# Eight heads to one bank of weighted values, and a new order of all engines with a period of one visit

## The chip, the core and the metric

The kernel runs on one core of a Trainium2 chip. The metric is the device time in microseconds (us) from the first to the last instruction; the median of three runs before the change is 2798.29 us. The engines are PE (TensorE, matmuls), ACT (ScalarE), DVE (VectorE), POOL (GpSimd) and SP (SyncE, which here only issues DMAs). Each works through its own instructions in program order and waits on semaphores.

## What is computed

A small network over x (4 batches, 512 tokens, 128 features): slot attention, a mixture of experts, six transformer layers and a quantised feed-forward block, each added to x. The change touches the six layers alone, and in them mostly the two attentions (16 heads of 8 features; 512 tokens on themselves, then on 77 context rows):

```python
def _attn(q, k, v, mask):
    scores = jnp.einsum('bqhd,bkhd->bhqk', q, k) / np.float32(np.sqrt(HD))
    scores = jnp.where(mask[:, None, None, :], jnp.float32(-jnp.inf), scores)
    w = jax.nn.softmax(scores, axis=-1)
    return jnp.einsum('bhqk,bkhd->bqhd', w, v)
...
for i in range(NL):
    xn = _adaln(x, noise_emb, n1_w[i], n1_b[i])
    ...
    a = _attn(q, k, v, src_mask).reshape(B, L, D) @ so_w[i].T
    x = x + a
    ...
    a = _attn(q, k, v, ctx_mask).reshape(B, L, D) @ co_w[i].T
    x = x + a
    xn = _adaln(x, noise_emb, n3_w[i], n3_b[i])
    h = jax.nn.gelu(xn @ f1_w[i].T + f1_b[i], approximate=False)
    x = x + (h @ f2_w[i].T + f2_b[i])
```

## The kernel before

The function `layers` (from L836) does the six layers for four batches: 24 visits, visit v being layer v // 4 and batch v % 4. One visit has, for the self-attention:

- "product query", "product key" (L1168): the rows of the normalised x times the weights, then DVE turns them (L1475), POOL and ACT split the float32 result into three bfloat16 parts (POOL "rotate" L1394, ACT "first" L1305, POOL "less" L1399, ACT "second" L1310, POOL "third" L1405). SP writes the parts to DRAM ("store", L651 to L661) and reads them back in another arrangement ("load pairs", L953 to L956: per half of the partitions the queries, the keys and the mask row) into `q6` and `k6`, which have two buffers, one for each of two neighbouring visits.
- "PE max" (L1039), 32 places of two matmuls each: scores with the queries on the rows, of which DVE takes the maximum of each row (L1450). The first of a visit waits for that visit's load of pairs. A group of four heads ("unit") has eight of them; POOL splits its maxima ("split", L1409 to L1412), PE turns them (L1105), ACT copies them (L1273) and SP puts them as rows into `q6` ("SP rows", L980).
- "PE exp" (L1050), 32 places of two matmuls: scores with the keys on the rows, less the maxima. ACT takes the exponential into `probs` (L1259).
- "PE pv" (L1086): four matmuls, one a head, of the weights times the values with a column of ones behind them. Each head writes 32 partitions of bank 6 (`pv_bank`), of which 9 hold something. After four such places a group of four heads is done: ACT copies the bank ("copy", L1267), PE turns it ("gather", L1122, four transposes), DVE inverts the sums and multiplies (L1482, L1487). There are four units a visit.
- "turn on", "project" (L1129, L1138), "DVE add" (L1493): the output projection.

The cross-attention has the same steps with 8 places of scores, 8 of maxima and 4 of "cross pv" (L1097, into bank 7, called `aux`), each of these with its own copy, gather and division. Then comes the feed-forward part ("up" L1192, "gelu" L1331, "down" L1201). Once a layer the keys of the context are made ("product context" L1168, "rope context" L1471, ... "store context"), and SP loads them with eight DMAs ("load context", L974), and the layer's weights come in.

The order of all engines is a table of numbers, `OFFSETS` (L674), one number for each place of an operation, repeated with the period `PERIOD` (here 15124 for two visits); `LAYER_OFFSETS` (L776) does the same once a layer. Every engine's instructions are written in rising order of these numbers, and semaphores make each wait for what it needs, so the table sets only the order on each engine. The same numbers, taken as times, hand out the buffers through `shared` (L824): three pairs of PSUM banks for the scores and products, three buffers of `probs` of four heads each (`QUAD_BUFFERS`), two of the copied bank.

## Time and profile before

| | before |
|---|---|
| median of three runs | 2798.29 us (2793.4 to 2815.2) |
| time of the profiled execution | 2804.61 us |
| its span, first to last instruction | 2802.5 us |
| PE busy | 2148.6 us (77%) |
| DVE busy | 1811.4 us (65%) |
| ACT busy | 1588.6 us (57%) |
| POOL busy | 907.6 us (32%) |
| mean granted clock of PE | 0.887 |

The first 550 us are slots, routing and experts, the last 155 the quantised block; neither is changed. The layers run from about 550 to 2645 us. In the page's 40 slices PE is busy nine tenths or more in nearly all of them from the tenth slice to the last but five, with a granted clock of nine tenths. A busy share is read as the time in which at least one matmul was under way; where two lines of a timeline overlap, the distance of their starts says what the first one cost. In a timeline the bracket at a line's end is the time that the engine stood idle before it, and what released it.

### The profile page before, as it was taken

What the parts mean: (1) busy time and instruction counts of PE and PEld (TensorE: products, weight loads), DVE (VectorE), ACT (ScalarE), POOL (GpSimd) and SP (SyncE); (2) the same over time, 40 slices, a digit from 0 to 9 for tenths busy, and PEclk for the clock granted to TensorE, in tenths of its full rate; (3) what the DMA queues carried; (4) which work ended last, traced back from release to release, by engine and by line L of the source; (5) the groups of instructions that cost most, each with busy time, mean ns of one, the idle gap of its engine ahead of it and who ended that gap; (6) DMA issues with size and microseconds to landing.
All of it is one profiled execution on the core that took longest, in us unless ns stands there. A gap on an engine that the chain in (4) does not pass through costs nothing. (4 is left out here: it accounts for less than half of the span.)

```text
span 2802.5 us, 40867 instructions
## 1 busy us (share of the span) xinstructions
PE 2148.6 (77%) x14402; PEld 947.5 (34%) x14402; DVE 1811.4 (65%) x3776; ACT 1588.6 (57%) x2003; POOL 907.6 (32%) x1951
## 2 busy tenths in 40 slices
PE   2444799637789988999899998999899998986312
PEld 1223466511233333333333333333333333332101
DVE  6777211335677776776777777777677777652398
ACT  2221233105577776677777776777677776773223
POOL 4110000032244344443443353444344343322133
PEclk9665899857899999999999999999999999997655
DMA  1000000022322332233333313332342223310000
GB/s 42 0 0 0 31 13 18 26 52 47 79 72 59 70 80 76 48 69 75 69 82 70 69 54 75 77 70 64 66 97 62 55 52 87 70 25 24 23 0 15
DMA packets 141019, 144.47 MB, mean 52 GB/s; under 512 B 30808, under 2 KB 122644, under 8 KB 140820
## 3 DMA queue, kind: packets, MB, share of 16 engines
q1 hardware_dynamic: 140831, 142.05, 22.1%
q8 instruction: 109, 1.79, 0.3%
q14 instruction: 79, 0.64, 0.1%
HBM read 79.01 MB, written 60.51 MB: 50 GB/s over the span
## 5 line engine op out<-in xcount | busy, mean ns | idle before, releaser
L1259 ACT ACTIVATE big<-ps 128x1024 f32<-128x1024 f32 x960 | 969.4, 1025 | 374.1 <-PE ps L1050 348.1
L1450 DVE TENSOR_REDUCE smax<-ps 128x2 f32<-128x1024 f32 x768 | 916.4, 1219 | 235.6 <-PE ps L1039 233.3
L1086 PE MATMUL ps<-big,vaug 128*32 128x512 f32 x3072 | 421.5, 621 | 4.0 <-ACT big L1259 3.8
L1039 PE MATMUL ps<-k,q 49*128 49x512 bf16 x1536 | 303.0, 398 | 156.1 <-DVE smax L1450 70.5
L1050 PE MATMUL ps<-q,k 52*128 52x512 bf16 x1536 | 305.0, 397 | 31.3 <-ACT big L1259 18.5
L1394 POOL TENSOR_TENSOR rot<-rot 128x512 f32<-128x512 f32 (+1 forms) x78 | 96.5, 1237 | 510.3 <-DVE rot L1471 366.5
L1039 PEld LDWEIGHTS ps<-k,q 49*128 49x128 bf16 x1536 | 73.2, 94 | 395.6 <-DVE smax L1450 148.4
L1457 DVE TENSOR_REDUCE maxima<-ps 128x8 f32<-128x616 f32 x192 | 149.3, 796 | 72.5 <-PE ps L1073 71.2
L1168 PE MATMUL ps<-xnT,w 128*128 128x512 f32 x288 | 167.5, 668 | 2.2 <-ACT xnT L1296 1.7
L624 DVE SCALAR_TENSOR_TENSOR state<-ps,share,state 128x128 f32<-128x128 f32 x128 | 36.0, 344 | 201.7 <-PE ps L595 201.7
L612 ACT ACTIVATE big<-ps 128x512 f32<-128x512 f32 x128 | 76.4, 597 | 144.3 <-PE ps L586 144.3
L1475 DVE TENSOR_TENSOR rot<-ps,cs 128x1024 f32<-128x1024 f32 x72 | 88.1, 1223 | 103.5 <-PE ps L1168 103.5
L1493 DVE TENSOR_TENSOR state<-state,ps 128x512 f32<-128x512 f32 x72 | 49.6, 688 | 154.4 <-PE ps L1201 98.6
L1050 PEld LDWEIGHTS ps<-q,k 52*128 52x128 bf16 x1536 | 75.4, 94 | 215.7 <-issue 77.4
L586 PE MATMUL ps<-xnT,big 128*128 128x512 f32 x256 | 119.0, 610 | 24.8 <-DMA big<-in_c_proj 24.8
L1409 POOL CAST mparts<-smax 128x16 bf16<-128x16 f32 x96 | 19.1, 199 | 362.7 <-DVE smax L1450 362.7
L1122 PE MATMUL ps<-ident,xnT 128*128 128x128 f32 x768 | 126.2, 288 | 11.9 <-ACT xnT L1267 8.8
L1267 ACT COPY xnT<-ps 128x512 f32<-128x512 f32 x192 | 112.5, 586 | 33.7 <-PE ps L1097 23.4
L1201 PE MATMUL ps<-w,big 128*128 128x128 f32 x768 | 126.5, 317 | 4.0 <-ACT big L1331 4.0
L595 PEld LDWEIGHTS ps<-big 128*128 128x128 f32 x1024 | 119.1, 192 | 14.3 <-issue 14.3
L595 PE MATMUL ps<-big 128*128 128x128 f32 x1024 | 119.2, 275 | 0.0
L1201 PEld LDWEIGHTS ps<-w,big 128*128 128x128 f32 x768 | 108.5, 219 | 29.3 <-issue 21.3
(274 smaller groups left out, 3252.5 us busy)
## 6 DMA issues: line engine op xcount, KB each, us to landing
q<-scratch_queries SPq DMA_DIRECT2D x48, 384.0 KB
k<-scratch_keys SPq DMA_DIRECT2D x48, 384.0 KB
cq<-scratch_cross_queries SPq DMA_DIRECT2D x48, 384.0 KB, 5.5
scratch_queries<-rparts SPq DMA_DIRECT2D x24, 384.0 KB, 2.3
scratch_keys<-rparts SPq DMA_DIRECT2D x24, 384.0 KB, 2.5
scratch_cross_queries<-rparts SPq DMA_DIRECT2D x24, 384.0 KB, 2.3
scratch_queries<-rparts SPq DMA_DIRECT2D x24, 256.0 KB, 2.6
scratch_keys<-rparts SPq DMA_DIRECT2D x24, 256.0 KB, 2.7
```

What stands on the lines that cost most here:

```text
L586: nc.tensor.matmul(m.ps[:, n % 4, :], m.fc[:, u, c * P:(c + 1) * P], m.xnT[:, b, :], start=True, stop=True).then_inc(h_ps, 1)
L595: last = nc.tensor.matmul(m.ps[:, 4 + i % 2, t * P:(t + 1) * P], m.hT[:, i % 2, c, t * P:(t + 1) * P], m.proj[:, u, c, :], start=(c == 0), ...
L1039: last = nc.tensor.matmul(out[:, u], m.q6[rows, v % 2, 2 * g + pr, qt * P:(qt + 1) * P], m.k6[rows, v % 2, 2 * g + pr, :], start=True, sto ...
L1050: last = nc.tensor.matmul(out[:, u], m.k6[rows, v % 2, 2 * g + pr, kt * P:(kt + 1) * P], m.q6[rows, v % 2, 2 * g + pr, :], start=True, sto ...
L1086: last = nc.tensor.matmul(m.ps[32 * j:32 * j + 32, pv_bank, :], m.vaug[:, v % 2, kt, 4 * g + j, :], of_quad("self", q)[:, j, :], start=(kt ...
L1122: last = nc.tensor.transpose(m.ps[:, aux, t * P:(t + 1) * P], m.unit[:, unit[kind, n], t * P:(t + 1) * P], m.ident[:])
L1168: got = nc.tensor.matmul(banks(kind, i)[:, half, 0:width(kind)], w_of(m, names[half]), rhs, start=True, stop=True)
L1201: last = nc.tensor.matmul(m.ps[:, aux, t * P:(t + 1) * P], m.hT1[:, c, t * P:(t + 1) * P], w_of(m, "f2")[:, c * P:(c + 1) * P], start=(c = ...
L1259: nc.scalar.activation(of_quad(kind, p // 2)[:, p % 2 * 2:p % 2 * 2 + 2, :], banks("exp" if kind == "self" else "cross exp", p), ACT.Exp, ...
L1267: nc.scalar.copy(m.unit[:, unit[kind, n], :], m.ps[:, pv_bank if kind == "self" else aux, :]).then_inc(u_sb[kind], 1)
L1450: nc.vector.tensor_reduce(m.smax[:, n % 2, qt, :, pr], banks("max", i), AX.X, ALU.max).then_inc(s_read["self"], 1)
L1457: nc.vector.tensor_reduce(m.maxima[:, qt, :, PAIRS // 2 * half:PAIRS // 2 * (half + 1)], banks("cross max", i)[:, :, 0:PAIRS // 2 * N_CTX] ...
```

## The change

Eight heads share the bank of weighted values. A head's own 32 columns are 16 zeros, 8 of values, the column of ones and 7 zeros. A head of an even group uses the 32 columns that begin at its values, so its result lies in rows 0 to 8 of 32 partitions and zeros are added to rows 16 to 31; a head of an odd group uses those that begin 16 before its values, so its result lies in rows 16 to 24. Both add into the same 32 partitions. So bank 6 is copied, turned and divided once for two groups: two units a visit in place of four, for the self-attention and the cross-attention alike. The rows of the projection weights `so` and `co` are permuted on the host to fit. The division works on twice as many columns.

`QUAD_BUFFERS` goes from 3 to 4, `hT1` gets memory of its own, and the context's keys get buffers of their own (`rot_c`, `rparts_c`, `left_c`); their product is made in two halves in bank `aux`, behind visit 0's first work and no longer ahead of everything. The period is one visit, 7218, and all numbers of the table are new.

```diff
-PERIOD_VISITS = 2
-PERIOD = 15124
+PERIOD_VISITS = 1
+PERIOD = 7218
 OFFSETS = {
...
     "PE max": (
-        -4847, -4662, -4608, -4142, -4025, -3873, -3726, -3639, -3501, -3362, -3205, -2802, -2623, -2444, -2265, -1004, -675, -555, -370,
...
+        -4361, -4115, -3949, -3669, -3607, -3448, -3299, -3248, -2981, -2752, -2226, -1995, -1972, -1842, -1644, -1514, -1042, -77, 114,
...
-    "ACT second key": (-6597, 903),
+    "ACT second key": (-5775,),
-    "SP load pairs": (-5986, 1514),
+    "SP load pairs": (-5161,),
...
-QUAD_BUFFERS = 3
+QUAD_BUFFERS = 4
+UNIT_PAIRS = GROUPS // 2
...
+    def of_head(values, block, g, j):
+
+        at = (block * HEADS + 4 * g + j) * 32 + 16 * (1 - g % 2)
+        return values[:, at:at + 32]
...
-                if kt == 0 and n >= 1:
-                    pe.wait_ge(u_sb["self"], n)
+                if kt == 0 and g % 2 == 0 and n >= 2:
+                    pe.wait_ge(u_sb["self"], n // 2)
                 for j in range(4):
-                    last = nc.tensor.matmul(m.ps[32 * j:32 * j + 32, pv_bank, :], m.vaug[:, v % 2, kt, 4 * g + j, :], of_quad("self", q)[:, j, :],
-                                            start=(kt == 0), stop=(kt == TB - 1))
+                    last = nc.tensor.matmul(m.ps[32 * j:32 * j + 32, pv_bank, :], of_head(m.vaug, v % 2 * TB + kt, g, j),
+                                            of_quad("self", q)[:, j, :], start=(kt == 0 and g % 2 == 0), stop=(kt == TB - 1 and g % 2 == 1))
...
             def copy_unit(kind, n):
-                act.wait_ge(pv[kind], TB * (n + 1) if kind == "self" else n + 1)
+                act.wait_ge(pv[kind], 2 * (n + 1) * (TB if kind == "self" else 1))
...
             def turn_on(kind, v):
-                pe.wait_ge(on[kind], GROUPS * (v + 1))
+                pe.wait_ge(on[kind], UNIT_PAIRS * (v + 1))
...
+            def context_products(half, n):
+                weights("context", n)
+                take_aux(x_read["context"], 2 * n + half + 1)
+                for k, name in enumerate(("ck", "ckr")):
+                    last = nc.tensor.matmul(m.ps[:, aux, k * N_HALF:(k + 1) * N_HALF], w_of(m, name),
+                                            m.ctxT[:, half * N_HALF:(half + 1) * N_HALF], start=True, stop=True)
+                last.then_inc(x_ps["context"], 1)
```

On PE, in the cross-attention of one visit in the middle of the layers, the program before has this order (`big,vcaug` is "cross pv", `ident,xnT` a gather, `cq,kc` and `q,k` scores for the exponential, `k,q` scores for the maxima):

```order
L1097 MATMUL ps<-big,vcaug 32x512 x4
L1039 MATMUL ps<-k,q 128x512 x2
L1061 MATMUL ps<-cq,kc 128x512 x2
L1122 MATMUL ps<-ident,xnT 128x128 x4
L1039 MATMUL ps<-k,q 128x512 x2
L1061 MATMUL ps<-cq,kc 128x512 x2
L1097 MATMUL ps<-big,vcaug 32x512 x4
L1039 MATMUL ps<-k,q 128x512 x2
L1061 MATMUL ps<-cq,kc 128x512 x4
L1122 MATMUL ps<-ident,xnT 128x128 x4
```

Every weighting is followed by its own gather, with scores between them. The same place of the changed program, on PE:

```order
L1103 MATMUL ps<-big,vcaug 32x512 x4
L1066 MATMUL ps<-cq,kc 128x512 x2
L1044 MATMUL ps<-k,q 128x512 x2
L1103 MATMUL ps<-big,vcaug 32x512 x4
L1044 MATMUL ps<-k,q 128x512 x2
L1055 MATMUL ps<-q,k 128x512 x2
L1128 MATMUL ps<-ident,xnT 128x128 x4
L1066 MATMUL ps<-cq,kc 128x512 x2
```

Two weightings share a gather; single pairs of scores still stand between them. On PE just ahead of the first maxima of a visit (the instruction that names `pairs_loaded`), before; here the semaphores that an instruction waits for stand behind it:

```order
L1050 MATMUL ps<-q,k 128x512 [waits max_read_self]
L1050 MATMUL ps<-q,k 128x512
L1039 MATMUL ps<-k,q 128x512 [waits probs_self]
L1039 MATMUL ps<-k,q 128x512
L1050 MATMUL ps<-q,k 128x512 [waits max_read_self]
L1050 MATMUL ps<-q,k 128x512
L1138 MATMUL ps<-w,on 128x128 [waits rows_copied_cross,weights_out]
L1138 MATMUL ps<-w,on 128x128 x3
L1039 MATMUL ps<-k,q 128x512 [waits max_read_self,pairs_loaded_0]
L1039 MATMUL ps<-k,q 128x512
L1050 MATMUL ps<-q,k 128x512 [waits probs_self]
L1050 MATMUL ps<-q,k 128x512
```

The first maxima stand behind the cross-attention's projection. The same place of the changed program, on PE:

```order
L1055 MATMUL ps<-q,k 128x512 [waits probs_self]
L1055 MATMUL ps<-q,k 128x512
L1144 MATMUL ps<-w,on 128x128 [waits rows_copied_cross,weights_out]
L1144 MATMUL ps<-w,on 128x128 x3
L1055 MATMUL ps<-q,k 128x512 [waits probs_self]
L1055 MATMUL ps<-q,k 128x512
L1091 MATMUL ps<-big,vaug 32x512 [waits probs_self]
L1091 MATMUL ps<-big,vaug 32x512 x3
L1044 MATMUL ps<-k,q 128x512 [waits max_read_self,pairs_loaded_0]
L1044 MATMUL ps<-k,q 128x512
L1055 MATMUL ps<-q,k 128x512 [waits probs_self]
L1055 MATMUL ps<-q,k 128x512
```

They stand one pair of scores and one weighting behind the projection; the wait for the pairs is on them in both. The third place is on ACT, from the second cast of the keys (`rparts<-hat`, "ACT second key"), before:

```order
L1259 ACTIVATE big<-ps 128x1024 [waits weighted_self,scores_cross]
L1310 CAST rparts<-hat 128x512 [waits less_high_key]
L1267 COPY xnT<-ps 128x512 [waits unit_turned_self,weighted_cross]
L1259 ACTIVATE big<-ps 128x1024 [waits scores_cross]
L1259 ACTIVATE big<-ps 128x1024 [waits weighted_self,scores_cross]
L1259 ACTIVATE big<-ps 128x1024 [waits scores_cross]
L1267 COPY xnT<-ps 128x512 [waits unit_turned_self,weighted_cross]
L1259 ACTIVATE big<-ps 128x1024 [waits weighted_cross,scores_cross]
```

The cast stands behind the second exponential of the cross-attention (`scores_cross`) and ahead of its four copies. On ACT in the changed program:

```order
L1270 ACTIVATE big<-ps 128x1024 [waits weighted_self,scores_cross]
L1278 COPY xnT<-ps 128x512 [waits unit_turned_self,weighted_cross]
L1270 ACTIVATE big<-ps 128x1024 [waits scores_self]
L1322 CAST rparts<-hat 128x512 [waits less_high_key]
L1270 ACTIVATE big<-ps 128x1024 [waits scores_cross]
L1270 ACTIVATE big<-ps 128x1024 [waits weighted_cross,scores_cross]
L1270 ACTIVATE big<-ps 128x1024 [waits scores_cross]
L1270 ACTIVATE big<-ps 128x1024 [waits weighted_cross,scores_self]
```

The cast has moved behind the first of the (now two) copies, deeper into the cross-attention, and less work stands between it and the first maxima.

## Rows read from the trace of the kernel before

**Rows 1.** Busy time by engine in the full part of the layers (us, instructions in brackets):

```profile
840.00:2500.00 1660.00, 1500.77 (x10850) 589.76 (x10848) 1214.76 (x2005) 1213.99 (x1483) 680.83 (x1620) 0.97 0.30 67
```

**Rows 2.** Waits of PE, 946 to 2391 us: us in total, times, longest:

```profile
PE ps L1039 <- DVE smax L1450: 44.9, 83, 1.6
PE ps L1039 <- DMA k<-scratch_neg_mask: 27.0, 9, 5.1
```

**Rows 3.** ACT's timeline, copies of the values of visits 5 and 23 (start, us, instruction):

```profile
946.96 0.59 ACT L1316 COPY vaug<-ps 128x512 f32<-128x512 f32 x1 [1.44 <-PE ps L1175]
...
2391.21 0.59 ACT L1316 COPY vaug<-ps 128x512 f32<-128x512 f32 x1 [1.44 <-PE ps L1175]
```

**Rows 4.** PE's timeline, five neighbours of one piece:

```profile
1207.94 0.39 PE L1050 MATMUL ps<-q,k 52*128 52x512 bf16 x2
1208.16 0.38 PE L1039 MATMUL ps<-k,q 49*128 49x512 bf16 x2
1208.47 1.07 PE L1086 MATMUL ps<-big,vaug 128*32 128x512 f32 x8
1209.47 0.66 PE L1122 MATMUL ps<-ident,xnT 128*128 128x128 f32 x4
1210.06 0.39 PE L1050 MATMUL ps<-q,k 52*128 52x512 bf16 x2
```

**Rows 5.** The page's groups of instructions: gathers on PE, copies on ACT:

```profile
L1122 PE MATMUL ps<-ident,xnT 128*128 128x128 f32 x768 | 126.2, 288 | 11.9 <-ACT xnT L1267 8.8
L1267 ACT COPY xnT<-ps 128x512 f32<-128x512 f32 x192 | 112.5, 586 | 33.7 <-PE ps L1097 23.4
```

**Rows 6.** Timelines, visit 9: second cast of keys, first load, first maxima:

```profile
1271.59 0.62 ACT L1310 CAST rparts<-hat 128x512 bf16<-128x512 f32 x1
...
1277.00 0.33 SPq L953 DMA_DIRECT2D q<-scratch_queries  x1
...
1290.25 0.39 PE L1039 MATMUL ps<-k,q 49*128 49x512 bf16 x2 [0.84 <-DMA k<-scratch_neg_mask]
```

**Rows 7.** Windows within that load; the last two columns are DMA share, GB/s:

```profile
1282.00:1284.00 2.00, 2.00 (x18) 1.08 (x12) 0.93 (x2) 0.90 (x1) 0.00 (x0) 1.00 1.13 155
```

**Rows 8.** Timelines, visit 8, whose first maxima follow no wait:

```profile
1195.38 0.62 ACT L1310 CAST rparts<-hat 128x512 bf16<-128x512 f32 x1
...
1214.20 0.39 PE L1039 MATMUL ps<-k,q 49*128 49x512 bf16 x2
```

**Rows 9.** Timelines, visit 10, with the context's load ahead of the pairs':

```profile
1352.46 0.62 ACT L1310 CAST rparts<-hat 128x512 bf16<-128x512 f32 x1
...
1358.41 4.91 SPq L974 DMA_DIRECT2D kc<-scratch_ctx_keys  x8
1363.43 0.41 SPq L953 DMA_DIRECT2D q<-scratch_queries  x1
...
1376.06 0.61 PE L1039 MATMUL ps<-k,q 49*128 49x512 bf16 x2 [4.83 <-DMA k<-scratch_neg_mask]
```

**Rows 10.** Windows after the waits of visits 1, 6, 10; third number from the end: clock:

```profile
662.00:672.00 10.00, 7.57 (x52) 1.90 (x52) 4.85 (x4) 4.71 (x6) 0.00 (x0) 0.83 0.01 2
1052.00:1062.00 10.00, 8.84 (x44) 2.68 (x44) 5.15 (x14) 4.88 (x6) 1.45 (x8) 0.68 0.02 3
1376.00:1386.00 10.00, 9.94 (x56) 3.25 (x60) 6.64 (x17) 5.81 (x7) 2.61 (x13) 0.83 0.01 3
```

**Rows 11.** Timelines, first work of the layers, first maxima, last visit's first maxima, last addition:

```profile
555.84 2.42 PE L1168 MATMUL ps<-ctxT,w 128*128 128x308 f32 x4 [21.69 <-DMA w<-in_w]
...
559.34 0.86 DVE L1505 BATCH_NORM_STATS2 bn_next<-state 128x6 f32<-128x128 f32 x4
...
600.87 1.46 PE L1039 MATMUL ps<-k,q 49*128 49x512 bf16 x6 [22.08 <-DMA k<-scratch_neg_mask]
...
2414.65 0.39 PE L1039 MATMUL ps<-k,q 49*128 49x512 bf16 x2 [0.59 <-ACT big L1259]
...
2644.21 0.69 DVE L1493 TENSOR_TENSOR state<-state,ps 128x512 f32<-128x512 f32 x1 [20.06 <-PE ps L1201]
```

More of the change, by code:

```diff
@@ L790 @@
[L790 to L799 removed]
+    "SP weights self": 3476,
+    "PE gain cross": 4223,
+    "DVE gain cross": 4268,
+    "SP weights out": 9987,
+    "SP weights ff": 13180,
+    "PE gain ff": 13780,
@@ new lines @@
+    "DVE gain ff": 13825,
+    "SP weights next": -10281,
+    "PE gain next": -8458,
+    "DVE gain next": -8413,
+    "PE context values": 10506,
+    "ACT copy context values": 10616,
+    "SP load context": 8933,
+    "SP weights context": 5188,
+    "PE product context 0": 6688,
+    "DVE rope context 0": 6773,
+    "PE product context 1": 7018,
+    "DVE rope context 1": 7103,
+    "POOL rotate context": 7198,
+    "ACT first context": 7358,
+    "POOL less context": 7458,
+    "ACT second context": 7598,
@@ L800 @@
+    "POOL third context": 7698,
+    "SP store context": 7838,
 }
```

339 lines of the change are left out of this document (167 added, 172 removed), and 21 rows, old and new, of the table OFFSETS.

## The prediction

> **What bounds the kernel now.** I read the busy shares first. In the full part of the layers PE is busy for 1500.8 of 1660 us, 90%, DVE and ACT for 73% each [rows 1]. So PE sets the pace, and what counts is what PE does and what it waits for. The copies of the values of visit 5 and visit 23 are 1444.25 us apart [rows 3], 18 visits, so a visit takes 80.24 us. The table has 75.62 for it (half of 15124, if its numbers count 10 ns; that they do is shown below).
>
> Then the waits of PE. In the 1445 us it stood for DVE's maxima 44.9 us in 83 small pieces, and 27.0 us in only 9 pieces for the DMAs of the pairs [rows 2]. The second kind matters here. After the second cast of the keys comes a fixed chain: last part, store, load, first maxima. In visit 9 the cast starts at 1271.59, SP issues the load at 1277.00 (5.41 later), and PE's first maxima come at 1290.25, 13.25 after the issue, with 0.84 of waiting [rows 6]. So the load takes some 13 us until PE may go on; while it runs the queues are full, a DMA share of 1.13 at 155 GB/s [rows 7]. In visit 10 it is 12.63 us from 1363.43 to 1376.06 [rows 9]. Cast to first maxima thus needs 5.41 + 12.6 to 13.25, so **18.0 to 18.7 us**. The table of before leaves 17.84 us between these two places in odd visits (2687 less 903, in units of 10 ns) and PE reached the place 18.66 - 0.84 = 17.82 us after the cast: the table's numbers are times of 10 ns, and PE keeps them where nothing holds it. Before, the load is just covered.
>
> Once a layer SP has the context's eight loads ahead (4.91 us to issue), the load goes out 10.97 us after the cast, and PE waits 4.83 us [rows 9].
>
> **The change part by part.**
>
> *Gathers.* 24 visits x 4 gathers fall away. One costs 0.59 us to the next start, and the pair of scores ahead of it 0.31 in place of 0.22 [rows 4]: 0.68 x 4 = 2.7 us of PE a visit. Over the program this is 65 us; the page's 126.2 us for 768 transposes give 63 for half of them [rows 5].
>
> *Matmuls side by side.* The extra 0.1 us is paid where scores (bfloat16, on half the rows) meet another kind. In the order there are 959 places on PE where scores are followed by something else, 876 after. That is 83 fewer, and the 96 gathers alone would remove up to 96. So the new order in itself saves nothing here.
>
> *ACT and DVE.* 96 copies of 0.586 us go [rows 5], and half of the inversions and products, whose remaining ones are twice as wide. Both engines have a quarter of their time free, so I price this at nothing; if ACT or DVE set the pace it would be worth 2.3 us a visit at the most.
>
> *More buffers, the context in two halves.* The fourth buffer of `probs` and the memory for `hT1` remove waits of ACT, which isn't the bound. The context's matmuls are 24 of half the width in place of 12. Nothing, either way.
>
> *The table.* 75.62 - 72.18 = 3.44 us a visit: 2.7 are the gathers, 0.7 tighter packing. I take all of it, since what made 80.24 of 75.62 (once-a-layer work that the period doesn't hold, the clock, waits) mostly stays.
>
> *What the table takes away.* It leaves 5775 - 4361 = 1414, 14.1 us, from the second cast of the keys to the first maxima, where 17.5 to 17.8 stood. The order says why this is real: between the scores of the exponential ahead of the cast and the first maxima, PE had 25 pairs of scores, 7 weightings, 4 gathers, a transpose group and a projection (visit 9), and now has 20, 6, 2, 1 and 1. By rows 4 that is 5 x 0.22 + 1.00 + 2 x 0.59 = 3.3 us less, 3.7 with the switches. The cast can't come earlier: it stands on ACT behind exponentials and a copy that wait for PE. Nor can the load: SP waits for the stores, as before. So the data are there 18.0 to 18.7 us after the cast and PE 14.1 us after: a **new wait of 3.9 to 4.6 us in every visit**. Visit 8 reached its place 18.82 us after the cast without waiting where the table had 17.50 [rows 8], 1.3 us late, so the wait may be as short as 2.6. I take 3.9. Everything of PE stands behind it, so ACT, DVE and POOL stop too.
>
> In the visit with the context's loads these can start once the last cross scores are done, 2.1 us after the cast by the table, plus an exponential, plus 4.9 of issuing: the pairs go out some 8 us after the cast, 2.6 later than in others. That wait is about 6.0. The mean is (3 x 3.9 + 6.0) / 4 = 4.4 us.
>
> *The clock.* In the 10 us behind such waits the mean granted clock was 0.83 (visit 1), 0.68 (visit 6) and 0.83 (visit 10, after 4.83 us of waiting) [rows 10]. It has two levels, 2.4 GHz (1.0) and 1.2 GHz (0.5), so it was at the lower one for 3.4, 6.4 and 3.4 us, in which half the work of PE is lost: 1.7 to 3.2 us. I take 2.1 a wait. The Trainium skill, "TensorE: Matmul & The Clock Gate", section "HAM oscillation — how this bites in real kernels", says that a kernel which waits for a DMA in every tile pays the fall of the clock in every tile. The trace agrees for these three waits.
>
> *Taken away with the old table.* The old waits: 4.8 and some 2.3 of clock a layer, and 0.3 a visit (3.4 us in four such pieces are what rows 2 hold beside the layers' 23.6): 2.1 a visit.
>
> A visit: 80.24 - 3.44 - 2.1 + 4.4 + 2.1 = **81.2 us**, 0.96 more. From the first maxima to those of the last visit there are 23 (600.87 to 2414.65 [rows 11]), so +22 us.
>
> *Ends.* The first statistics of the layers stood behind the context's product and its turning, until 559.34 [rows 11]; now they don't: between nothing and the 9 us since the stage began, I take 5 (the product alone is 2.42). From the last visit's first maxima to the last addition the table has 259.1 us and now 246.9; measured are 230.3 [rows 11], so 12.2 x 0.89 = 11 us fewer.
>
> **Sum.** 2804.6 (the profiled execution) - 5 + 22 - 11 = 2810.6. The median lies 6.3 below that execution: **2804 us**. About 1% is what a measurement of this kernel can tell from no change, that is 2770 to 2826.
>
> **Rivals.**
>
> *The load stays hidden: faster.* Then a visit is 80.24 - 3.44 - 2.1 = 74.7 us and the program 2798 - 16 - 23 x 5.5 = 2655 us. It needs PE to be 4 us late between cast and maxima, or a load of under 9 us. Against it: the load took 12.6 us or more with full queues [rows 7, 9]. Chance 0.15. The Trainium skill, "DMA: Bandwidth & Descriptors", section "Anatomy of one DMA — SWDGE (gpsimd) path", fits a DMA as 2.0 us and its bytes at 436 GB/s. The four large loads of 48x8x512 bfloat16 are 1.57 MB: an estimate of 5.6 us by that page, which would be hidden. The trace has 13 and less than half that rate.
>
> *The wait comes, but cheaper: faster.* It is 2.6 to 3.5 us long, the clock mostly holds, or PE's later waits for DVE and ACT shrink by as much since these have caught up. A visit is 80.24 - 5.54 + 3.4 to 4.4, so 78.1 to 79.1, and the program 2733 to 2756. For it: 45 us of small waits for maxima [rows 2]. Against it: PE keeps the table's distances (17.82 us against 17.84), so they hold little slack to win back. Chance 0.2.
>
> *A second wait: slower.* SP's rows of maxima for the third unit now stand 3.0 us (3288 to 3588) ahead of the scores that need them, where 5.2 stood. If these small DMAs take 4 us or more and land behind the pairs' traffic, PE waits another 1 us a visit; with the full 3.2 of clock and waits of 4.8 a visit is 80.24 - 5.54 + 4.8 + 3.2 + 1.0 = 83.7 and the program 2798 - 16 + 23 x 3.5 = 2862. It decides from a rows' landing of 3.0 us on. Chance 0.15.
>
> **How the numbers follow.** The forecast as summed has 0.5, with its own range of 2770 to 2850 (wait 2.9 to 4.6, clock 1.7 to 3.2). Of it 0.35 lie within 1% and 0.15 above. Faster by over 1%: 0.15 + 0.2 = 0.35. Within 1%: 0.35. Slower by over 1%: 0.15 + 0.15 = 0.30. The range 2725 to 2855 holds the forecast and the cheaper wait and leaves out the hidden load and most of the second wait.
>
> **What will show it.** Right: PE's wait for `k<-scratch_neg_mask` has some 24 pieces of 3 to 6 us, near 100 us in all; the first maxima come 12.5 to 13.3 us after the load's issue; the clock is at 0.5 behind most of them; gathers are 384 transposes, 63 us; visits are 80 to 82 us apart. Wrong: such waits under 1.5 us (the load was hidden, or PE late for another reason), visits of 75 us, or a large wait for the DMA of the rows of maxima.

## The result and the profile after

| | before | after |
|---|---|---|
| median of the runs, us | 2799.5 (20 runs, 2789.2 to 2815.2) | 2784.4 (20 runs, 2777.5 to 2797.1) |
| ratio, 95% interval | 1 | 0.9945 [0.9932, 0.9958] |
| profiled execution, us | 2802.5 | 2776.6 |
| mean granted clock | 0.887 | 0.868 |
| copies of values, visit 5 to 23, us | 1444.25 | 1444.35 |

The changed kernel is 0.55% faster: inside the range and inside "within 1%", but on the other side of no change than the forecast of 2804. The steady visit came out at the 80.24 us of before, where I had 81.2. That it is the same to the hundredth is an accident of sums that cancel, as the experiments show; the gain lies at the two ends.

The groups of instructions for gathers and for the copies that feed them (line, engine, operation | busy us, mean ns | idle before). They answer to [rows 5]:

```profile
L1128 PE MATMUL ps<-ident,xnT 128*128 128x128 f32 x384 | 62.2, 285 | 14.4 <-ACT xnT L1278 8.8 <-ACT mct L1290 5.6
L1278 ACT COPY xnT<-ps 128x512 f32<-128x512 f32 x96 | 56.4, 588 | 26.1 <-PE ps L1091 17.9 <-PE ps L1103 8.2
```

Half of both is gone: 384 transposes, 62.2 us, as forecast (63).

PE's waits, 978 to 2423 us, the 18 visits from 5 to 23 (in total, times, longest), against [rows 2]:

```profile
PE ps L1044 <- DMA k<-scratch_neg_mask: 105.5, 18, 9.2
PE ps L1044 <- DVE smax L1460: 21.8, 36, 0.9
PE ps L1111 <- DVE on_rows L1499: 18.0, 18, 1.0
```

The new wait is there, once in each of the 18 visits, 5.9 us in the mean (forecast 4.4). But the small waits for DVE's maxima, 44.9 us in 83 pieces before, are 21.8 in 36, and two more of before, 946 to 2391 us, are gone from this list, the scores' waits for ACT's gelu and for its exponentials:

```profile
PE ps L1039 <- ACT big L1331: 13.7, 27, 0.8
PE ps L1050 <- ACT big L1259: 12.8, 40, 0.6
```

Without the waits for the load PE was idle for 112.0 us in these 18 visits before (139.0 less 27.0) and for 59.4 us after (164.9 less 105.5). One new small wait has come: the turn of maxima stands right behind a gather and waits 1.0 us for DVE's products.

One such wait, visit 11. Timelines of ACT, SP and PE (start, us):

```profile
1425.85 0.61 ACT L1322 CAST rparts<-hat 128x512 bf16<-128x512 f32 x1
...
1428.66 0.51 SPq L661 DMA_DIRECT2D scratch_keys<-rparts  x1
...
1433.24 0.32 SPq L958 DMA_DIRECT2D q<-scratch_queries  x1
...
1446.04 0.61 PE L1044 MATMUL ps<-k,q 49*128 49x512 bf16 x2 [6.37 <-DMA k<-scratch_neg_mask]
```

PE reached the place at 1446.04 - 6.37 = 1439.67, 13.82 us after the cast (forecast 14.1), and the load took 12.80 us from its issue (forecast 12.6 to 13.25). What I had too short in this visit is the way from cast to load: 7.39 here, 5.41 in my sum. The windows over this wait (PE busy, clock, DMA share, GB/s):

```profile
1442.00:1444.00 2.00, 0.00 (x0) 0.99 1.13 144
1444.00:1446.00 2.00, 0.00 (x0) 0.50 0.22 29
1446.00:1448.00 2.00, 1.97 (x8) 0.50 0.00 0
1448.00:1450.00 2.00, 2.00 (x11) 0.50 0.00 0
1450.00:1452.00 2.00, 2.00 (x12) 0.80 0.01 4
```

PE stands, the clock falls from 2.4 to 1.2 GHz, and PE's work begins at the lower one and keeps it for some 5 us. In the 2 us behind each of the 18 waits the mean granted clock was 0.50 to 0.55, and 8 us behind them it was back at 1.00.

The first and the last visit's first maxima and the last addition, against [rows 11]:

```profile
594.27 1.46 PE L1044 MATMUL ps<-k,q 49*128 49x512 bf16 x6 [25.44 <-DMA k<-scratch_neg_mask]
...
2407.84 0.60 PE L1044 MATMUL ps<-k,q 49*128 49x512 bf16 x2 [6.01 <-DMA k<-scratch_neg_mask]
...
2618.30 0.69 DVE L1505 TENSOR_TENSOR state<-state,ps 128x512 f32<-128x512 f32 x1 [18.50 <-PE ps L1210]
```

Head: 600.87 to 594.27, 6.6 us earlier (forecast 5). Between the two first maxima: 1813.6, before 1813.8. Tail: 210.5 us where 229.6 stood, 19.1 less (forecast 11).

### The profile page after: what moved, and what is told of

It reads as the page before. It is cut to its first block and busy times, and to the rows that moved or that the text cites. A ratio compares the mean times of both kernels' runs of the same rounds, so it can differ in the third digit from the quotient of the medians.

```text
span 2776.6 us, 39486 instructions
## 1 busy us (share of the span) xinstructions
PE 2102.3 (76%) x14041; PEld 910.0 (33%) x14042; DVE 1790.8 (64%) x3584; ACT 1526.3 (55%) x1907; POOL 906.5 (33%) x1951
## 5 line engine op out<-in xcount | busy, mean ns | idle before, releaser
L1270 ACT ACTIVATE big<-ps 128x1024 f32<-128x1024 f32 x960 | 947.7, 1023 | 383.2 <-PE ps L1055 358.8
L1044 PE MATMUL ps<-k,q 49*128 49x512 bf16 x1536 | 310.2, 407 | 194.8 <-DMA k<-scratch_neg_mask 155.1
L1091 PE MATMUL ps<-big,vaug 128*32 128x512 f32 x3072 | 427.5, 636 | 2.1 <-ACT xnT L1278 1.8
L1406 POOL TENSOR_TENSOR rot<-rot 128x512 f32<-128x512 f32 x72 | 91.4, 1269 | 186.9 <-DVE rot L1476 186.8
L1390 POOL TENSOR_TENSOR tmp_next<-rstd_next 128x4 f32<-128x4 f32 x72 | 14.2, 198 | 365.5 <-DVE rstd_next L1529 361.8
L1210 PE MATMUL ps<-w,hT 128*128 128x128 f32 x768 | 129.0, 321 | 2.4 <-ACT hT L1343 2.4
L1284 ACT COPY mt<-ps 12x512 bf16<-12x512 bf16 x96 | 55.1, 574 | 130.5 <-PE ps L1111 130.5
L1210 PEld LDWEIGHTS ps<-w,hT 128*128 128x128 f32 x768 | 109.9, 221 | 44.8 <-issue 40.4
L595 PEld LDWEIGHTS ps<-big 128*128 128x128 f32 x1024 | 119.1, 192 | 14.3 <-issue 14.3
L1416 POOL TENSOR_TENSOR rparts<-hat,rparts 128x512 bf16<-128x512 f32 x72 | 83.4, 1158 | 113.3 <-ACT rparts L1322 113.3
L1410 POOL TENSOR_TENSOR hat<-rot,rparts 128x512 f32<-128x512 f32 x72 | 83.5, 1160 | 110.6 <-ACT rparts L1318 110.6
```

The source lines that it names most:

```text
L595: last = nc.tensor.matmul(m.ps[:, 4 + i % 2, t * P:(t + 1) * P], m.hT[:, i % 2, c, t * P:(t + 1) * P], m.proj[:, u, c, :], start=(c == 0), ...
L1044: last = nc.tensor.matmul(out[:, u], m.q6[rows, v % 2, 2 * g + pr, qt * P:(qt + 1) * P], m.k6[rows, v % 2, 2 * g + pr, :], start=True, sto ...
L1091: last = nc.tensor.matmul(m.ps[32 * j:32 * j + 32, pv_bank, :], of_head(m.vaug, v % 2 * TB + kt, g, j), of_quad("self", q)[:, j, :], start ...
L1210: last = nc.tensor.matmul(m.ps[:, aux, t * P:(t + 1) * P], m.hT1[:, c, t * P:(t + 1) * P], w_of(m, "f2")[:, c * P:(c + 1) * P], start=(c = ...
L1270: nc.scalar.activation(of_quad(kind, p // 2)[:, p % 2 * 2:p % 2 * 2 + 2, :], banks("exp" if kind == "self" else "cross exp", p), ACT.Exp, ...
L1406: nc.gpsimd.tensor_tensor(x[:, 0, :], x[:, 0, :], x[:, 1, :], ALU.add).then_inc(x_rot[kind], 1)
```

## The experiments

Times are medians; ratios are against the kernel before, run on the same chip in the same job, so they compare across jobs. "Visit" is the distance of ACT's copies of values from visit 5 to visit 23, by 18. PE busy and idle and the mean granted clock are of those same 18 visits. With the merge that is the same work of PE in every kernel but `fill` and the padded ones, which add some.

| run | median us | ratio [95%] | visit us | PE busy, idle us | clock |
|---|---|---|---|---|---|
| before | 2799.5 | 1 | 80.24 | 1305.2, 139.0 | 0.97 |
| after | 2784.4 | 0.9945 [0.9932, 0.9958] | 80.24 | 1279.5, 164.9 | 0.93 |
| later300 | 2763.3 | 0.9847 [0.9818, 0.9877] | 79.81 | 1284.8, 151.8 | 0.95 |
| later600 | 2710.3 | 0.9661 [0.9630, 0.9691] | 77.02 | 1261.4, 125.0 | 0.98 |
| half_load | 2628.0 | 0.9370 [0.9342, 0.9398] | 72.94 | 1242.5, 70.4 | 0.98 |
| fill | 2760.6 | 0.9827 [0.9781, 0.9872] | 79.00 | 1305.6, 116.3 | 0.96 |
| split4 | 2619.1 | 0.9356 [0.9320, 0.9392] | 73.20 | 1242.2, 75.4 | 0.98 |
| before_split4 | 2756.5 | 0.9829 [0.9779, 0.9879] | 78.43 | 1297.7, 114.0 | 0.98 |
| ctx_after | 2768.0 (one run) | none | 79.41 | 1281.8, 147.6 | 0.94 |
| merge_old_table | 2841.3 | 1.0130 [1.0090, 1.0171] | 82.74 | 1308.4, 181.0 | 0.94 |
| merge2 | 2880.9 | 1.0275 [1.0231, 1.0318] | 84.29 | 1312.2, 205.0 | 0.93 |
| merge2_split4 | 2830.9 | 1.0086 [1.0053, 1.0119] | 82.49 | 1302.8, 182.1 | 0.94 |
| merge3_split4 | 2768.2 | 0.9882 [0.9862, 0.9902] | 79.48 | 1273.6, 157.0 | 0.96 |
| merge3_pad | 2801.1 | 1.0002 [0.9987, 1.0018] | 80.28 | 1299.7, 145.4 | 0.97 |
| split4_pad | 2653.8 | 0.9460 [0.9436, 0.9485] | 74.96 | 1280.1, 69.3 | 0.98 |
| split2 | 2597.4 | 0.9265 [0.9231, 0.9299] | 72.36 | 1242.1, 60.4 | 0.98 |
| best1 | 2591.3 | 0.9245 [0.9211, 0.9280] | 71.89 | 1234.8, 59.2 | 0.99 |
| best2 | 2601.9 | 0.9278 [0.9253, 0.9304] | 72.43 | 1242.4, 61.4 | 0.98 |

### Is the wait for the load paid, or do other waits take its place?

Theory A says that the wait is paid in full; theory B, that without it other waits would stand in its place. First the place of the maxima was moved, in the table only. `later600` (`later300` alike with some 280 units):

```diff
     "PE max": (
-        -4361, -4115, -3949, -3669, -3607, -3448, -3299, -3248, -2981, -2752, -2226, ...
+        -3750, -3524, -3344, -3087, -3026, -2829, -2724, -2668, -2529, -2416, -2073, ...
-    "POOL split": (-3002, -1323, 1636, 2753),
+    "POOL split": (-2402, -1323, 1636, 2753),
```

> The changed kernel with only the first ten blocks of maxima of a visit placed later: 0 to 7 by about 280 units (3.2 us at 80.24 us per 7218 units), 8 by 180, the reading on DVE, the first split on POOL with them; nothing else is moved. Their place on PE comes after other matmuls of the period, so that PE reaches the wait for the loaded pairs later. Theory A (the wait of 5.8 us for the load is paid in full in each visit, and a clock loss behind it): the wait shrinks by about 3 us in 23 visits, 2784 - 70 = about 2715, and less if the clock stays up. Theory B (PE's waits are interchangeable: what the load wait does not take, waits for DVE's reading or for the exponentials take, as the 80.24 us per visit both kernels show suggests): within 10 us of 2784.

> The same with the first eight blocks of maxima placed about 590 units (6.5 us) later, and 8 to 10 by 450, 340 and 150, so that they stand close together. Theory A: the load wait (mean 5.8 us in 18 visits, 6.7 to 9.2 us in the context visits) is all but gone except in the visits that load the context; 23 x 5.8 = 133 us, with the clock after the wait (about 2 us a visit) up to 180: 2600 to 2650. Theory B: the maxima, now packed, wait for DVE's reading (1.2 us each) instead: within 15 us of 2784.

PE's waits of later600, visits 5 to 23:

```profile
PE ps L1036 <- DVE smax L1452: 44.7, 54, 1.3
PE ps L1047 <- DVE smax L1452: 19.9, 18, 1.1
PE ps L1036 <- DMA k<-scratch_neg_mask: 8.1, 7, 2.1
```

The load wait went from 105.5 to 8.1 us and the clock from 0.93 to 0.98, yet the visit gave back 3.2 us, not 7: maxima that stand close together wait for DVE's reading, 64.6 us where 21.8 stood, and a matmul of the feed-forward part ("down") waits 13.6 us for ACT's copy of the turned maxima. In later300 the load wait fell by 43 us, but 14.3 us of waits for an exponential and 7 for DVE came, PE was busy 5 us more, and the visit gained 0.4. Neither theory is right alone: the wait is paid, and this way of hiding it costs half or more of its worth. The next run leaves the order alone and makes the load shorter.

```diff
-                    sp.dma_start(m.q6[lo:lo + ROW_MASK, i], src[u]).then_inc(loaded[i], 16)
+                    few = PAIRS if v < 2 else PAIRS // 2
+                    sp.dma_start(m.q6[lo:lo + ROW_MASK, i, 0:few], src[u][:, 0:few]).then_inc(loaded[i], 16)
...
-                    sp.dma_start(m.k6[lo:lo + ROW_MASK, i], src[u]).then_inc(loaded[i], 16)
+                    sp.dma_start(m.k6[lo:lo + ROW_MASK, i, 0:few], src[u][:, 0:few]).then_inc(loaded[i], 16)
```

> The changed kernel with the order untouched, but from the third visit on each of the four large transfers of queries and keys moves pairs 0 to 3 only, half of its bytes; pairs 4 to 7 keep what an earlier visit left, so this part of the attention is computed on old data. Theory A: the load, 12.3 to 13.3 us from issue to first maxima, takes about 7.5 us; the wait of 5.8 us falls to 1 or less in ordinary visits: 22 x 5 = 110 us, 2670, less still with the clock. Theory B: the wait disappears, and the time stays within 15 us of 2784.

2628 us, ratio 0.937, even below theory A's figure: a visit almost without the wait takes 72.94 us, where my sum had 74.7. PE's waits of half_load, visits 5 to 23:

```profile
PE ps L1037 <- DVE smax L1453: 21.8, 36, 0.9
PE ps L1104 <- DVE on_rows L1492: 18.0, 18, 1.0
PE ps L1037 <- DMA k<-scratch_neg_mask: 11.0, 6, 3.0
```

The small waits are those of the changed kernel to the tenth: the long wait didn't cover or shrink them, it stood beside them. Theory B falls.

`fill` asks for the clock's part:

```diff
+FILL = 11
...
+                out = free_banks("max", i)
                 if i % PER_VISIT == 0:
+                    if v >= 2:
+                        for k in range(FILL):
+                            for u in range(2):
+                                rows = slice(u * ROW_BLOCK, u * ROW_BLOCK + ROWS_MAX)
+                                nc.tensor.matmul(out[:, u], m.q6[rows, 1 - v % 2, k % PAIRS, 0:P], m.k6[rows, 1 - v % 2, k % PAIRS, :],
+                                                 start=True, stop=True)
                     pe.wait_ge(loaded[v % 2], 96 * (v // 2 + 1))
```

> The changed kernel with 11 pairs of matmuls more ahead of each wait for the load (22 of 49 x 128 by 512 columns, about 4.5 us a visit), repeating maxima of the visit before into the bank that the first maxima then overwrite: PE is busy in the time in which it waited. It tells the clock's share from the wait's. If the lower clock behind the wait costs 2.1 us a visit as I took it (23 visits): 2784 - 45 = about 2740, with the granted clock over the steady stretch up from 0.93 to 0.97. If the clock would have fallen anyway, or what it costs is hidden by other waits: 2780 to 2800, the fill costing a little in the visits where it runs past the load.

It gained 1.2 us a visit without making anything else shorter; the clock rose from 0.93 to 0.96, and 56.5 us of the wait stayed, 3.1 a time. So work that nobody reads buys back part of the clock's cost, about half of what I forecast; half of the wait was still there, and with it a stretch at the lower clock.

`split4` is `half_load` without leaving anything out, and `before_split4` the same edit in the kernel before:

```diff
+FIRST_PAIRS = 4
...
+                for part, done in ((slice(0, FIRST_PAIRS), loaded[i]), (slice(FIRST_PAIRS, PAIRS), late[i])):
+                    for u in range(2):
...
+                        sp.dma_start(m.q6[lo:lo + ROW_MASK, i, part], src[u][:, part]).then_inc(done, 16)
...
+                        sp.dma_start(m.k6[lo:lo + ROW_MASK, i, part], src[u][:, part]).then_inc(done, 16)
...
+                if i % PER_VISIT == FIRST_PAIRS // 2 * PER_UNIT:
+                    pe.wait_ge(late[v % 2], 64 * (v // 2 + 1))
```

> The changed kernel with each load of pairs cut in two: the pairs 0 to 3 of queries and keys and the mask first, then pairs 4 to 7, each part with a semaphore of its own; the first maxima wait for the first part, the maxima of group 2 (about 50 us later) for the second. All bytes move, the computation is whole, the order on the engines is untouched. Theory A, by the run with half of the load (72.9 us a visit, first maxima no longer late): the wait of 5.8 us goes in the same way; the four issues more on SP's queue and the second half's traffic beside it take a little back: 2630 to 2660. Theory B (it was the halved traffic of that run, less contention for all transfers, that made it fast): 2720 to 2780.

> The kernel before with the same cut of the load in two. Its table gives the load 18.0 to 18.7 us, and PE waited for it 27.0 us in 9 of 18 visits. If the load was nearly hidden there, the cut is worth these waits and the clock behind them, 30 to 40 us: 2799 - 35 = about 2765. If cutting the load helps by itself, in traffic or for SP's queue, it gains as much as in the changed kernel, 120 us or more.

2619 us with all bytes moved: what PE paid for was the time until the first pairs are there. The windows over the 18 visits of after and of split4 (PE, PEld, DVE, ACT, POOL busy, clock, DMA share, GB/s):

```profile
978.31:2422.66 1444.35, 1279.50 (x9137) 490.08 (x9136) 1044.05 (x1605) 1008.59 (x1221) 602.40 (x1420) 0.93 0.33 70
```

```profile
939.51:2257.12 1317.61, 1242.19 (x9137) 481.97 (x9136) 1043.27 (x1605) 1006.15 (x1221) 604.48 (x1420) 0.98 0.35 77
```

The same 9137 matmuls in the same order. Of the 126.7 us between the two, 89.4 are idle time of PE (the load wait went from 105.5 to 15.5) and 37.3 are PE busy longer with the same work, at a mean granted clock of 0.93 in place of 0.98. That is 5.0 us of wait and **2.1 us of clock** for each visit, the price that I had taken from three windows. `split2` below, in which 1.0 us of the load wait is left, has 5.8 and 2.1: the whole new wait costs 7.9 us a visit. In the kernel before the same cut gave 1.8 us a visit (forecast of the old wait: 2.1) and 1.7%, no more.

The Trainium skill, "TensorE: Matmul & The Clock Gate", section "HAM oscillation — how this bites in real kernels", says that a kernel which waits for a DMA in each tile pays a throttled stretch behind each wait; its example has 1.67 us of it, half of that lost. This trace agrees on the mechanism, 18 times in 18 visits, and has 2.1 us lost each time.

```diff
-    "SP load context": 8933,
+    "SP load context": 9400,
```

> The changed kernel with the load of the context's keys, eight transfers, placed 225 units later, behind the load of pairs of the same visit in place of ahead of it. Theory A (the waits of 6.7 to 9.2 us in visits 6, 14, 18 and 22 are longer by the context's transfers ahead of the pairs): these fall to 4 to 6 us, the sum of the waits in 18 visits from 104 to about 93 us, the time by 10 to 15 us. Rival: they stay as they are, since the stores and the load of the cross queries, not the context, hold the queues.

PE's waits of ctx_after, visits 5 to 23:

```profile
PE ps L1036 <- DMA k<-scratch_neg_mask: 88.2, 18, 6.3
```

From 105.5 to 88.2 us, the longest from 9.2 to 6.3. In the five visits that load the context the wait fell from 8.1 to 5.1 us in the mean; in the other 13 it stayed near 5. It was the context's transfers. The time is of one run only and has no interval.

### What are the gathers worth, and what the new order?

The merge alone: the changed kernel with the old table, of which each pair's second place was kept for copy, gather and division.

```diff
-PERIOD_VISITS = 1
-PERIOD = 7218
+PERIOD_VISITS = 2
+PERIOD = 15124
...
```

> The merge alone: the changed kernel (eight heads into one bank, half of the copies, gathers and divisions) under the table of the kernel before, in a period of two visits, with the second place of each pair kept for copy, gather and division; one first block of the context's weighted values and the two products of the context stand a little elsewhere, since they share the auxiliary bank. There the load has 18 us and is waited for 1.5 us a visit. Theory A, my sum's term: 2.7 us of PE a visit for the gathers that fall away, in 24 visits: 2800 - 62 = about 2740, still 80.24 - 2.7 = 77.5 us a visit. Rival: the gathers lay in time in which PE would have waited for DVE or ACT anyway: within 15 us of 2800.

> The merge alone under the table of the kernel before, as in the run merge_old_table, with the load cut in two as in split4 and the context's two products placed so that neither waits for the other's reading (in merge_old_table PE waited 1.7 us there, and its clock was 0.50 for 10 us behind it, once in four visits). Beside the kernel before with the cut load (2756 us, 78.4 us a visit) it is the merge without any load wait. If the gathers' 2.7 us of PE a visit are worth their time when nothing stalls: 2756 - 62 = about 2695. If they only turn into other waits under this table: within 15 us of 2756. What is left to 2619 us, the changed kernel with the cut load, is then the new table's.

> The merge alone under the old table with the whole load in one, and the context's products placed as in merge2_split4. If the misplaced context products made merge_old_table slow (2841 us; the visits with them took 86.6 us in place of 81.0, so 6 x 5.6 = 34 us), this gives about 2805, no faster than the kernel before; if my term of 2.7 us a visit holds besides, about 2745.

All three are slower than the kernel before or than its version with the cut load. The misplaced context products don't explain it as I thought: at the new places of merge2,

```diff
-    "PE product context 0": -17520,
+    "PE product context 0": -17420,
...
-    "PE product context 1": -17225,
+    "PE product context 1": -16690,
```

it got worse (2881 against 2841 us). PE now waited 11.2 us in 4 pieces for the reading of these products, 9.5 in 8 before: in the auxiliary bank each half holds up the bank's next user. The scores' waits for exponentials grew more, from 17.6 to 36.9 us, the longest from 1.0 to 5.2. Windows of merge2_split4 at one place, PE idle and the clock lower behind it (PE busy, clock, DMA share, GB/s):

```profile
1281.77:1285.77 4.00, 3.47 (x26) 1.00 0.66 210
1285.77:1289.77 4.00, 2.09 (x14) 0.73 1.06 190
1289.77:1293.77 4.00, 4.00 (x18) 0.50 1.15 171
```

These windows led me to theory C: gathers that fall away turn into waits and a lower clock. For a clean test the context's products went back to the ring of banks and their old places, and in the padded kernels as much work as the gathers had was put in:

```diff
-                take_aux(x_read["context"], 2 * n + half + 1)
+                if half == 0:
+                    free_banks("context", n)
...
-                    last = nc.tensor.matmul(m.ps[:, aux, k * N_HALF:(k + 1) * N_HALF], w_of(m, name),
+                    last = nc.tensor.matmul(banks("context", n)[:, half, k * N_HALF:(k + 1) * N_HALF], w_of(m, name),
...
+            def pad():
+                if reader[0] is not None:
+                    pe.wait_ge(*reader[0])
+                for t in range(TB):
+                    nc.tensor.transpose(m.ps[:, aux, t * P:(t + 1) * P], m.ident[:], m.ident[:])
...
+                if kt == TB - 1 and g % 2 == 0:
+                    pad()
...
+                if g % 2 == 0:
+                    pad()
```

> The merge alone under the old table with the load cut in two, as merge2_split4, but the context's products keep their ring bank and their old places, so that the context visits (84.5 us there against 73.8) are as in the kernel before with the cut load (2756 us). My term: the gathers are worth 2.7 us a visit, about 2695. Theory C, from the trace of merge2_split4 (at a place where two gathers stood, PE now waited 2.1 us more for DVE's readings, and the clock fell to 0.50 to 0.73 for 5 us behind it): the old table has DVE and ACT one step behind PE, so gathers that fall away turn into waits and lower clock, 2750 to 2790.

> merge3_split4 with the PE work of the removed gathers put back: four transposes of 128 x 128 of the identity into the auxiliary bank behind the last weighted values of the first unit of each pair, and ahead of the first of the context's, 4 x 4 transposes a visit, read by nobody. My term: 2.7 us a visit dearer than merge3_split4, +62 us. Theory C: no dearer, 10 to 40 us cheaper if the clock stays up, back to about 2756.

> The changed kernel with the load cut in two (split4, 2619 us) and the same 4 x 4 transposes a visit put back. It measures what the gathers are worth under the new table, where PE hardly waits. My term: 2.7 us of PE a visit, 24 visits, +60 to +65 us, 2680. Theory C holds here too if the time stays under 2635.

merge3_split4 has a ratio of 0.9882 [0.9862, 0.9902], before_split4 0.9829 [0.9779, 0.9879]: the merge alone gains nothing. But the pad costs 33 us under the old table and 29 to 35 us under the new one (by the ratios and by the medians). By these totals alone the gathers would be worth something in both orders, half of the 65 us that I had, and theory C would fall, since nothing came back with the pad. The timelines say otherwise: the pad does not stand where the gathers stood. PE behind the copy of the values of visit 7, in before_split4,

```profile
1091.52 0.38 PE L1046 MATMUL ps<-k,q 49*128 49x512 bf16 x2
1091.98 0.63 PE L1129 MATMUL ps<-ident,xnT 128*128 128x128 f32 x4
1093.23 0.39 PE L1046 MATMUL ps<-k,q 49*128 49x512 bf16 x2 [0.62 <-DVE smax L1457]
```

in merge3_split4,

```profile
1095.65 0.38 PE L1044 MATMUL ps<-k,q 49*128 49x512 bf16 x2
1097.36 0.39 PE L1044 MATMUL ps<-k,q 49*128 49x512 bf16 x2 [1.33 <-DVE smax L1461]
```

and in merge3_pad:

```profile
1105.27 0.66 PE L1086 MATMUL ps<-ident 128*128 128x128 f32 x4
...
1107.08 0.38 PE L1044 MATMUL ps<-k,q 49*128 49x512 bf16 x2
1108.79 0.39 PE L1044 MATMUL ps<-k,q 49*128 49x512 bf16 x2 [1.33 <-DVE smax L1471]
```

In all three the second maxima come 1.71 us behind the first, since PE waits for DVE's reading. The gather ran inside this wait; taken away, it left the wait longer by 0.71 us and the time the same. The pad (`ident`) stands ahead of the weighting, where PE waits for nothing, and left the wait as it was. Over the 18 visits 52 of the 144 gathers of before_split4 stand directly ahead of a wait of scores for DVE's reading of maxima, and 20 of the 72 of merge3_split4; of the pads none does, and under the new table no gather does. PE's waits for these readings rose from 49 to 76 us from before_split4 to merge3_split4, and the clock went from 0.98 to 0.96. So theory C holds at these places, some 32 of the 72 gathers that went, and the pad didn't test it: it measures what four transposes cost where PE is moving. What the other 40 were worth was not followed up.

In the steady visits that is 0.8 us under the old table (79.48 to 80.28) and 1.8 us under the new one (73.20 to 74.96). There PE was busy 37.9 us longer for 72 pads, 0.53 us each, and idle 6.1 us less, mostly since the load wait fell from 15.5 to 6.9.

So the merge, which takes four gathers a visit away, gets no time back under the old table: PE is busy 24.1 us less in the 18 visits and idle 43.0 us more. PE's groups of scores, 950 to 2230 us of before_split4 (| busy, mean ns | idle before, releasers):

```profile
L1057 PE MATMUL ps<-q,k 52*128 52x512 bf16 x1046 | 204.2, 389 | 16.1 <-ACT big L1266 12.1 <-DVE smax L1457 2.3
L1046 PE MATMUL ps<-k,q 49*128 49x512 bf16 x1046 | 201.5, 387 | 60.5 <-DVE smax L1457 39.2 <-ACT big L1338 12.4 <-ACT big L1266 5.4
```

the same of merge3_split4:

```profile
L1055 PE MATMUL ps<-q,k 52*128 52x512 bf16 x1034 | 205.4, 396 | 21.3 <-ACT big L1271 15.9 <-DVE smax L1461 4.3
L1044 PE MATMUL ps<-k,q 49*128 49x512 bf16 x1032 | 201.6, 392 | 79.7 <-DVE smax L1461 62.0 <-ACT hT L1344 12.6 <-DVE maxima L1468 2.5
```

and of split4:

```profile
L1051 PE MATMUL ps<-k,q 49*128 49x512 bf16 x1114 | 218.3, 394 | 37.3 <-DVE smax L1467 21.4 <-DMA k<-scratch_neg_mask 15.5
L1062 PE MATMUL ps<-q,k 52*128 52x512 bf16 x1118 | 210.8, 390 | 0.1
```

Idle time ahead of scores: 76.6 us, 101.0 with the merge under the old table, 37.4 under the new table, 15.5 of it the rest of the load. This is what the new order does: its scores come when DVE and ACT have freed their banks. Over 18 visits the table takes 81.6 us of idle time (157.0 to 75.4) and 31.4 us of busy time, at a clock of 0.98 in place of 0.96: 6.3 us a visit, and 149 us from merge3_split4 to split4. How much of the busy time is the clock and how much is matmuls that stand better side by side, no run separates. Nor did a run put the gathers back into their own places, so the table's and the merge's shares stay bound to each other: a gather is worth something only where the order lets PE go on.

### A version that beats both

`split2` is split4 with `FIRST_PAIRS = 2`. best1 is split4 and best2 is split2, both with

```diff
-    "PE turn maxima": (-2251, -1008, 3138, 3525),
-    "ACT copy maxima": (-2037, -954, 3210, 3570),
-    "SP rows": (-1959, -876, 3288, 3648),
-    "SP load context": 8933,
+    "PE turn maxima": (-2051, -1008, 3138, 3525),
+    "ACT copy maxima": (-1867, -954, 3210, 3570),
+    "SP rows": (-1789, -876, 3288, 3648),
+    "SP load context": 9400,
```

> As split4, but cut behind pairs 0 and 1: a quarter of the bytes first, and the maxima of group 1, about 15 us later, wait for the rest. If what is left of the wait in split4 (15.5 us in 8 of 18 visits, up to 5.4) is the first part's transfer, it goes: about 2600. If the rest now comes too late for group 1, or the smaller transfers are no quicker, 2620 to 2640.

> The changed kernel with the load cut in two, the load of the context's keys behind that of the pairs, and the first turn of maxima of a visit 200 units later (with its copy and its rows), so that it does not stand right behind a gather whose division it must wait for (18 waits of 1.0 us). From 2619 us: the turn's wait 18 to 24 us less if PE has nothing else to wait for, the context's order another 5: 2590 to 2605. Rival: the auxiliary bank's next user waits instead, 2615 to 2620.

> The changed kernel with the load cut behind pairs 0 and 1 (split2, 2597 us), the context's load behind that of the pairs and the first turn of maxima later (which with the cut in halves gave 2591 against 2619). If both gains add up: 2565 to 2575. If they took away the same waits: 2588 to 2597.

best1 (the load in halves, the context's load behind the pairs', the turn later) is at 2591 us, 0.9245 [0.9211, 0.9280], 7.5% faster than before; split2 is at 2597, with 1.0 us in one piece left of the wait for the pairs. The two gains don't add: best2 is at 2602. The intervals of the three overlap, so no order between them is shown. By its trace PE waits there 6.2 us in 5 pieces, up to 2.5, for rows of maxima, and 16.9 us in 18 pieces for the copy of the turned maxima, which now holds the auxiliary bank when the feed-forward part's "down" needs it. The second wait is in best1 as well, the first is 1.7 us there.

## Why the prediction was wrong, point by point

**The new wait: the mechanism right, the size too small.** Place, frequency and distance (13.82 us in every one of the 18 visits, forecast 14.1) are as forecast; the wait is 5.9 us a visit, not 4.4. In the 13 visits that don't load the context it is 5.0 us, where I had 3.9. There the step that failed is "5.41 later", from cast to load, which I took from one visit: it is 6.1 us in the mean, 5.4 in six visits and up to 7.5 in the others, where the last key store lands later (below); the load itself took 12.3 to 13.8, about as forecast. In the five visits that load the context the wait is 6.7 to 9.2 us, 8.1 in the mean, where I had 6.0. Cast to load is 7.7 to 8.4 there, as I said, but the load behind the context's transfers took 12.8 to 15.0 us, where I had 12.6 to 13.25 for every visit. My own terms gave 6.5, too: 3.9 and the 2.6 by which the load goes out later.

**The clock: right.** 2.1 us a wait forecast, 37.3 / 18 = 2.1 measured. Wait and clock together are 80.24 - 72.36 = 7.9 us (after and split2), forecast 6.5.

**The old waits: right.** 80.24 - 78.43 = 1.81, forecast 2.1.

**The gathers: nearly right under the new table, worth nothing under the old one.** I gave each its distance to the next start, 0.59 us and the dearer switch, 2.7 us a visit. As a pad under the new table they are 0.53 us of PE's busy time each, 2.1 us a visit. Under the old table the merge alone made a visit 1.05 us longer (78.43 to 79.48). The distance to the next start is what a gather costs where PE goes on at once; ahead of a wait for another engine, as at the place shown above, it costs nothing, and I didn't ask which of the 96 stood there.

**"So the new order in itself saves nothing here": the step that failed.** I counted switches of kind on PE, found no fewer than the gathers explain, and gave the table 0.7 us of tighter packing; of the rest I wrote that "what made 80.24 of 75.62 ... mostly stays". It didn't. Merge and table together are worth 78.43 - 72.36 = 6.1 us a visit with the load wait away in both (before_split4 and split2), where I had 3.44. Half of it, 3.1 us, is PE's busy time, gathers above all; the other half, 3.0 us, is PE's small waits for DVE, ACT and POOL (114.0 us of idle time to 60.4), a term that my sum put at nothing. The largest of them, 45 us for DVE's maxima, was in [rows 2], and I used it only in a rival, against which I said that these waits hold little slack. With all terms: -1.8 - 6.1 + 7.9 = 0.0 measured, -2.1 - 3.4 + 6.5 = +1.0 forecast. The measured three close by themselves, being the steps of one way from before to after; the misses are what counts: 2.6 us too little for order and merge, 1.4 too little for wait and clock, 0.3 too much for the old waits. Two large errors in opposite directions left 1 us a visit, 22 us in all, and this put the sign wrong. That the time still lies within 1% of the forecast is luck.

**The ends: mis-sized.** 6.6 us for 5 and 19.1 for 11. Under the old table the merge alone shortens the tail from 230.7 to 221.1 us (first maxima of visit 23 to the last addition, before_split4 and merge3_split4), so some 10 of the 19 may be the merge's, which my ratio of table lengths didn't hold; the other 9 I didn't follow up.

**The rivals.** The hidden load came out false for this kernel and its time of 2655 too high: with the wait taken away it is 2597 (split2). That later waits would shrink because of the stall is false: 21.8 us of waits for maxima with the stall and without. A second wait for the rows of maxima didn't come; none is in the changed kernel's list of PE's waits over these visits, down to 1.4 us.

## What to carry to other kernels

A new order has to be priced by the waits it removes as well as by the work it moves: take the list of PE's small waits and ask for each whether its two places still stand as close together. An instruction that stands ahead of a wait for another engine gives nothing back when it goes; look at what follows it before you price it by its length. When a transfer bounds a step, ask first which part of it the first consumer needs; a second semaphore was worth 165 us here, eleven times what the whole change had brought. And a stall is dearer than it is long: here 5.8 us of it cost 7.9, since the work behind it began at half the clock.

## What the runs showed of the hardware

A store can land late with the queues nearly empty. In visit 11 the last key store, 128 KB, was issued at 1428.66, and the load that waits for it at 1433.24. The three stores of keys among the transfers issued from 1420 to 1450 us (KB each, us to landing):

```profile
scratch_keys<-rparts SPq DMA_DIRECT2D x1, 384.0 KB, 2.5
scratch_keys<-rparts SPq DMA_DIRECT2D x1, 256.0 KB, 2.9
scratch_keys<-rparts SPq DMA_DIRECT2D x1, 128.0 KB, 4.5
```

The smallest one took the longest, and in the 2 us before the load the DMA share was 0.02:

```profile
1432.00:1434.00 2.00, 2.00 (x16) 1.00 0.02 4
```

In visit 9 the load followed 2.6 us behind the same store. One thing that differs is code loading. In visits 11, 12, 13, 22 and 23, where this store took 4.0 to 4.6 us to land, the profile has a transfer of the instruction queue q8 in the stretch from 1.5 us before the store's issue to the load's. In the twelve visits without any instruction transfer there the store took 2.5 to 2.7, also in the two of them where the load went out only 4.8 us behind it. But in visit 1 there is such a transfer and the store took 2.2. No run varied it, so it goes together in this trace and is not shown as the cause. The Trainium skill, "DMA: Bandwidth & Descriptors", section "Anatomy of one DMA — SWDGE (gpsimd) path", puts the fixed cost of a DMA mostly into the completion, which is held back until the data are written, "especially when the write target is HBM". The row has the landing long after the data moved, as the page has it; but the section is about DMAs that GpSimd issues, these stores are SP's, and it doesn't tell why the same store takes 2.5 us in one visit and 4.5 in another.

The load's time can be read as a fixed part and a rate. In visit 11 the whole load (1.57 MB) let PE go 12.8 us after its issue in the changed kernel; in split4's visit 11 the first part (0.79 MB, the rest behind it) took 7.4, in half_load's, with nothing behind it, 6.9. By an estimate from these differences the second half costs 5.4 to 5.9 us, 133 to 145 GB/s, and 1 to 2 us are fixed; the windows of [rows 7] and of the wait above have 155 and 144 GB/s.
